# Opening and closing parts of two attention stages over several PSUM banks

## The reference

```
q, k, v = projections of x, 16 heads of 64
scores  = q . k * scale   (+ causal mask in the first, + rel_bias[bucket(key - query)] in the third)
attn    = softmax(scores)
out     = sum over heads of W_O . (attn . v)
x       = layernorm(x + out)
```

## Time and profile before

| what | value |
|---|---|
| median of 3 runs | 4450.3 us (4441.75 to 4450.66) |
| profiled execution | 4442.77 us, its span 4441.0 us |
| TensorE, VectorE, ScalarE, GpSimd busy | 87%, 73%, 43%, 66% of the span |
| mean granted TensorE clock | 0.944 of full |
| s0 with its weights | 0 to 1230 us |
| gated stage | 1233 to 2619 us |
| s2 with its weights | 2623 to 4302 us |
| expert stage | 4305 to 4441 us |

### The profile page before, as it was taken

How to read it: one execution, slowest core, us unless ns; L and a number is a source line. 1 busy time by engine, 2 the same in 40 slices (tenths; PEclk the granted TensorE clock), 3 DMA queues, 4 the chain that set the end, 5 groups by cost and what they waited for, 6 DMA issues and landing times. The chain is left out here.

```text
span 4441.0 us, 63434 instructions
## 1 busy us (share of the span) xinstructions
PE 3881.5 (87%) x22554; PEld 2209.9 (50%) x22554; DVE 3243.7 (73%) x5656; ACT 1923.2 (43%) x3478; POOL 2937.1 (66%) x2164
## 2 busy tenths in 40 slices
PE   5998998999868889889899847999999999999964
PEld 3555555555445555555555423555455445545523
DVE  3786877868577787777876627888788788878826
ACT  1443443444345455455455312444344444434423
POOL 0776775757626777877887833777677677767740
PEclk6999999999979999999999957999999999999987
DMA  3000000000020000100000021122212221212111
GB/s 53 14 14 14 24 14 24 18 6 6 1 75 27 19 28 27 37 19 28 32 28 10 6 62 25 29 38 35 39 29 40 32 40 29 42 24 41 19 53 33
DMA packets 98041, 125.90 MB, mean 28 GB/s; under 512 B 28896, under 2 KB 76448, under 8 KB 97728
## 3 DMA queue, kind: packets, MB, share of 16 engines
q1 hardware_dynamic: 97728, 121.86, 12.5%
HBM read 103.69 MB, written 18.12 MB: 27 GB/s over the span
## 5 line engine op out<-in xcount | busy, mean ns | idle before, releaser
L776 POOL TENSOR_TENSOR s_psum_p<-s_psum_p,s_prob 128x1024 f32<-128x1024 f32 (+3 forms) x640 | 1335.6, 2087 | 388.3 <-ACT s_prob L511 338.3
L511 ACT ACTIVATE s_prob<-s_sT 128x1024 f32<-128x1024 f32 (+2 forms) x896 | 791.6, 931 | 877.2 <-DVE s_sT L658 495.1
L412 PE MATMUL s_pv<-s_prob,s_vp 128*64 128x512 f32 (+3 forms) x3584 | 797.7, 566 | 3.9 <-POOL s_prob L761 3.9
L614 DVE CUSTOM_DVE_ANT_0 s_mx<-s_mx,s_strip 128x512 f32<-128x512 f32 x640 | 429.6, 712 | 177.2 <-PE s_mx L371 174.7
L1670 POOL TENSOR_TENSOR s_psum_p<-s_psum_p,s_prob 128x1024 f32<-128x1024 f32 x192 | 462.1, 2407 | 104.7 <-ACT s_prob L1393 102.6
L1393 ACT ACTIVATE s_prob<-s_sT 128x1024 f32<-128x1024 f32 x256 | 262.4, 1025 | 581.9 <-PE s_sT L1257 581.9
L371 PE MATMUL s_mx<-s_bh,s_ah 64*128 64x512 f32 (+3 forms) x1792 | 412.1, 455 | 110.3 <-DVE s_bm L604 48.3
L663 DVE RECIPROCAL s_recip<-s_recip 128x128 f32<-128x128 f32 x512 | 452.4, 921 | 35.2 <-ACT s_recip L459 35.2
L776 POOL TENSOR_TENSOR s_psum_p<-s_prob 128x1024 f32<-128x1024 f32 (+1 forms) x128 | 288.0, 2250 | 236.2 <-ACT s_prob L511 233.5
L604 DVE TENSOR_REDUCE s_bm<-s_mx 128x8 f32<-128x1024 f32 (+3 forms) x384 | 367.4, 957 | 54.6 <-PE s_mx L371 45.7
L371 PEld LDWEIGHTS s_mx<-s_bh,s_ah 64*128 64x128 f32 x1792 | 171.9, 188 | 466.6 <-issue 192.1
(11 more groups left out here) (251 smaller groups left out, 7395.6 us busy)
## 6 DMA issues: line engine op xcount, KB each, us to landing
s_strip<-bias_rows SPq DMA_DIRECT2D x256, 144.0 KB, 5.7
s_wr<-gated_weights SPq DMA_DIRECT2D x32, 960.0 KB, 4.8
s_near<-bias_rows SPq DMA_DIRECT2D x256, 48.0 KB, 2.0
x<-s_x SPq DMA_DIRECT2D x12, 512.0 KB, 3.2
s_x<-x SPq DMA_DIRECT2D x8, 512.0 KB, 5.1
gated_weights<-s_side_hi SPq DMA_DIRECT2D x8, 480.0 KB, 2.6
gated_weights<-s_side_lo SPq DMA_DIRECT2D x8, 480.0 KB, 2.9
s_x<-in_L_attn_x_dram SPq DMA_DIRECT2D x4, 512.0 KB, 4.3
```

The source lines that it names most:

```text
L412: last = mm(pv[heads(hd), lo:CH], vp[:, g % 2, j, heads(hd)], prob[:, k % PR, hd, lo:CH], start=j == 0, stop=end)
L511: nc.scalar.activation(prob[:, k % PR, :, lo:CH], sT[:, k % 2, :, lo:CH], ACT.Exp, scale=st.scale).then_inc(exp_done, 1)
L614: last = nc.vector.tensor_tensor_reduce(out=mx[:, hd, :], in0=mx[:, hd, :], in1=strip[:, g % 2, hd, first:first + CH], scale=1.0, scalar=N ...
L776: nc.gpsimd.tensor_tensor(out[:, :, lo:CH], src, p[:, :, lo:CH], ALU.add)\
```

## The change

- `bank_of` gives the first jobs banks of their own: xt and v of pair 0 use `misc` and `pv`, the four items of pair 0 the four banks of `sT`; these don't wait for a free `misc`. In the closing y uses two banks of `sT` and t the two others.
- `chunk_bank`: the maxima of pair 0 rotate over `mx` and the two halves of `sT`. TensorE may be three chunks ahead of VectorE.
- The order of the opening: v of pair 0 comes after three maxima, the items of pair 1 after maxima 4, 6, 8 and 10. A first scores job waits until all maxima are read.
- y of the last batch waits for the normalization only before its last pair of heads.
- The closing's layer norm goes in two halves (`half_norm`, `half_scale`, two roots, two stores).
- The x loads of the first two batches are issued in the weights block: in s0 before the bias store, whose landing the block no longer waits for (ScalarE waits for it before copying z of pair 7, and SP at the end of the stage); in s2 before the load of `wo`.
- `recycle` only notes the semaphores; `clear` clears those of the gated stage in the weights block of s2. The blocks that only cleared are gone.

```diff
+        def bank_of(job):
+            kind, of, k = (job + (0,))[:3]
+            if of == 0 and kind in ("xt", "v"):
+                return (misc, pv)[k][:, :]
+            if of == 0 and kind == "item":
+                return sT[:, k // 2, k % 2, :]
+            if of == B - 1 and kind in ("y", "t"):
+                return sT[:, 0 if kind == "y" else 1, k, :]
+            return misc[:, :]
+
+        def chunk_bank(g, n):
+            return mx[:, :, :] if g > 0 or n % 3 == 0 else sT[:, n % 3 - 1, :, :]
...
-                misc_free()
-                before = job
+                out = bank_of(job)
+                if job[0] in ("y", "t") and job[1] == B - 1:
+                    pe.wait_ge(exp_done, GP * U)
+                elif job[0] not in ("xt", "item", "v") or job[1] > 0:
+                    misc_free()
+                    before = job
...
                 elif kind == "y":
-                    if k == 0:
+                    if of < B - 1 and k == 0:
                         pe.wait_ge(z_done, 2 * NPAIR * (of + 1))
                     for p in range(NPAIR):
-                        last = mm(misc[:, :], wo[:, p, :], z[:, (of * NPAIR + p) % NZ, half(k)],
+                        if of == B - 1 and p == NPAIR - 1:
+                            pe.wait_ge(z_done, 2 * GP - 1 + k)
+                        last = mm(out, wo[:, p, :], z[:, (of * NPAIR + p) % NZ, half(k)],
                                   start=p == 0, stop=p == NPAIR - 1)
...
-                pe.wait_ge(mx_read, NMX * g + n)
+                if g > 0:
+                    pe.wait_ge(mx_read, NMX * g + n)
+                elif n >= 3:
+                    pe.wait_ge(mx_read, n - 2)
+                elif n > 0:
+                    pe.wait_ge(lo_done, 2 * n)
...
                 if k >= 2:
                     pe.wait_ge(exp_done, k - 1)
+                else:
+                    pe.wait_ge(mx_read, NMX)
...
-            for k in range(2):
-                misc_job(("v", 0, k))
             for n in range(NMX):
                 maxima(0, n)
-                if n < 4:
-                    misc_job(("item", 1, n))
+                if n == 2:
+                    for k in range(2):
+                        misc_job(("v", 0, k))
+                    pe.wait_ge(v_done, 2)
+                if n in (4, 6, 8, 10):
+                    misc_job(("item", 1, n // 2 - 2))
...
+                if st.causal and s == 2 * (NZ - 2):
+                    act.wait_ge(rows_stored, 16)
...
+            def half_norm(h):
+                part = slice(4 * h, 4 * h + 4)
+                x, square = x2[:, (B - 1) % 2, part, :], yT[:, half(h)].rearrange("p (i d) -> p i d", d=D)
+                mean, var = sums[:, 0, part], sums[:, 1, part]
+                dve.wait_ge(res_done, 2 * (B - 1) + h + 1)
+                nc.vector.tensor_reduce(mean, x, X, ALU.add).then_inc(end_step, 1)
...
+            def half_scale(h):
...
-            for n in range(7):
-                layer_norm(B - 1, n)
+                half_norm(c)
+            for c in range(2):
+                half_scale(c)
...
-            root(B - 1)
+            for h in range(2):
+                root(B - 1 + h, slice(4 * h, 4 * h + 4))
...
-            store(B - 1)
-            sp.wait_ge(x_stored, 16 * B)
+            for h in range(2):
+                sp.wait_ge(end_done, h + 1)
+                sp.dma_start(x_rows(x_out, B - 1)[:, 4 * h:4 * h + 4, :], x2[:, (B - 1) % 2, 4 * h:4 * h + 4, :])\
+                    .then_inc(x_stored, 16)
+            sp.wait_ge(x_stored, 16 * (B + 1))
...
+                for b in range(2):
+                    load(sp, b)
                 sp.wait_ge(b_copied, 4)
                 sp.dma_start(tables, rows.unsqueeze(1).to_broadcast([H, ROWS, TAB])).then_inc(b_stored, 16)
-                sp.wait_ge(b_stored, 16)
             else:
+                for b in range(2):
+                    load(sp, b)
                 sp.dma_start(wo[:, :, :], w["Wo"].rearrange("(t p) d -> p t d", p=P)).then_inc(loaded, 16)
+                cst.clear(sp)
...
     def recycle(self, used):
-        with self.nc.Block() as block:
-            @block.sync
-            def _(sp):
-                for sem in used:
-                    sp.sem_clear(sem)
-        self.spent += used
+        self.pending = used
+
+    def clear(self, sp):
+        for sem in self.pending:
+            sp.sem_clear(sem)
+        self.spent += self.pending
+        self.pending = []
```

More of the change, by code:

```diff
@@ L328, in misc_job @@
                     side, c, cols = 2 * (k // 2), k % 2, slice(p * P, (p + 1) * P)
-                    mm(misc[:, :], wab[:, side, cols], xh[:, half(c)], start=True, stop=False)
-                    mm(misc[:, :], wab[:, side, cols], xl[:, half(c)], start=False, stop=False)
-                    mm(misc[:, :], wab[:, side + 1, cols], xh[:, half(c)], start=False, stop=True)\
+                    mm(out, wab[:, side, cols], xh[:, half(c)], start=True, stop=False)
+                    mm(out, wab[:, side, cols], xl[:, half(c)], start=False, stop=False)
+                    mm(out, wab[:, side + 1, cols], xh[:, half(c)], start=False, stop=True)\
                         .then_inc(ab_full, 1)
@@ L344, in misc_job @@
                     for n in range(4):
-                        last = nc.tensor.transpose(misc[:, n * P:(n + 1) * P], x2[:, of % 2, 4 * k + n, :],
+                        last = nc.tensor.transpose(out[:, n * P:(n + 1) * P], x2[:, of % 2, 4 * k + n, :],
                                                    cst.ident[:, :])
@@ L358, in misc_job @@
                         i = 4 * k + n
-                        last = nc.tensor.transpose(misc[:, n * P:(n + 1) * P], yT[:, i * P:(i + 1) * P],
+                        last = nc.tensor.transpose(out[:, n * P:(n + 1) * P], yT[:, i * P:(i + 1) * P],
                                                    cst.ident[:, :])
@@ L449, in _ @@
             misc_job(("rs", 2 * GP - 1))
[L450 to L453 removed]
+            for kind in ("y", "t"):
+                for c in range(2):
+                    misc_job((kind, B - 1, c))
         @block.scalar
@@ L477, in misc_job @@
                     dst = ah if k < 2 else bh
-                    copy(dst[:, of % 3, half(k % 2)], misc[:, :]).then_inc(hi_done, 1)
+                    copy(dst[:, of % 3, half(k % 2)], src).then_inc(hi_done, 1)
                 elif kind == "v":
@@ L489, in misc_job @@
                         act.wait_ge(v_full, 2 * NPAIR * of)
-                    copy(xh[:, half(k)], misc[:, :]).then_inc(xh_done, 1)
+                    copy(xh[:, half(k)], src).then_inc(xh_done, 1)
                 elif kind == "y":
@@ L495, in misc_job @@
                         act.wait_ge(ln_step, LN * of)
-                    copy(yT[:, half(k)], misc[:, :]).then_inc(yT_done, 1)
+                    copy(yT[:, half(k)], src).then_inc(yT_done, 1)
             def exponentials(k):
@@ L847, in raw_weights @@
                         .then_inc(raw_in, 16)
-            for b in range(2):
-                load(b)
             for g in range(GP):
@@ L1764, in gated_stage, with attention_weights @@
         return used
-def attention_weights(nc, cst, st, w, wab, wv, wo, scratch, sT, bias, banks):
+def attention_weights(nc, cst, st, w, wab, wv, wo, scratch, sT, bias, banks, load):
     with ExitStack() as ctx:
@@ L1864, in _ @@
                     .then_inc(lo_cut, 1)
+    return b_stored if turn else None
 def expert_stage(nc, cst, w, x_in, out):
```

68 lines of the change are left out of this document (42 added, 26 removed).

## The result

| | before | changed kernel |
|---|---|---|
| median | 4450.5 us (4441.8 to 4451.1) | 4350.8 us (4348.2 to 4356.8) |
| span of the profiled execution | 4441.0 us | 4349.2 us |
| mean granted TensorE clock | 0.944 | 0.955 |

The ratio is 0.978, with an interval of 0.9767 to 0.9794: the change makes the kernel 98 us faster (92 to 104). Between the two profiled executions it is 91.8 us, against 89 forecast, and the profiled execution of before was one of its fastest.

The account below looks back on a forecast made before the run. TensorE bounds the long middle of a stage; openings and closings are bound by waits between instructions. Terms 14.5 + 19.6 + 1.5, 8.9, 8.5, 0.9 + 24.5 + 1.5, 8.9 sum to 89 us: 4354 or 4361, predicted 4358, range 4342 to 4382.

Parts of the forecast that it names:

- Start of s0: Before s0's first transpose: without the bias-table wait and with x loaded early, it comes at 23.7 instead of 38.16, gaining 14.5 us.
- Opening of s0: First transpose to pair 0's last maximum in s0: six banks make it 32.5 instead of 52.1 us, gaining 19.6.
- Clock: Openings of s0 and s2: four gapless items may raise TensorE to full clock for v; 0 to 3 us each, 1.5 taken.
- Opening of s2: First transpose to pair 0's last maximum in s2: 38.0 instead of 62.5 us, gaining 24.5, plus 1.5 for the clock.
- Closings: Ends of s0 and s2: earlier y and fewer copy waits bring the first addition 8.1 us earlier; 8.9 each with the store.
- The 1.2 for an earlier rise of the clock: Closings of s0 and s2: TensorE, busy since the rowsum product, reaches full clock sooner in y, saving about 1.2 us.
- Clearing: Between stages: dropping the semaphore-clearing blocks saves 2.5, 3.5 and 2.5 us, sum 8.5; 50 clears cost some 3 us if uncovered.
- Start of s2: s2's weights block: x ahead of wo delays the cast 3.3 us, yet the transpose comes at 2640.4 instead of 2641.39, gaining 0.9.
- Pairs: Steady loop over pairs in s0 and s2: each pair's jobs unchanged, TensorE-bound, so nothing gained or lost.
- covers fail: Rival, 0.15: delays by W_O, strips, clock, root, stores and small stalls cost up to 19 us together; 70 gained, 4377.
- More: Rival, 0.07: both openings at full clock throughout, items also twice as fast (2.5 each); 98 us or more gained, 4344.
- The clock swings between banks: Rival, 0.04: closings over four banks stay at half clock, losing 5.0 each, openings miss 3; 61 us gained, 4386.

Follow-up runs that it names:

- the last run above: Changed kernel with, in s2's opening, x loads behind wo, pair 0's strips issued in the weights block and 17 spare TensorE matmuls: ratio 0.978, median 4351.4 us.

## Why the prediction came out right, and where its steps were off

- **Start of s0**, 14.5: right in size (14.36), right in part in cause. The wait is 10.8, x itself 3.5. W_O did not wait for x: its landing took 7.9 us before and after, and its last cut stands at 22.20 instead of 21.67. That the first transpose is at 23.80 as forecast is in part luck: the weights end 0.5 us later, and the change of blocks takes 0.6 us where I took 1.
- **Opening of s0**, 19.6 + 1.5: it gained 24.3. The step that was off is VectorE's share. I took the 17.3 us of work and *added* 25 gaps; in the rows of the changed kernel most instructions that wait for nothing start 0.08 us before the modelled end of the one before them (a reduction behind the addition of the mask 0.03 after it), so that 17.6 us of durations, added up one by one, cover 16.50 us. In the rows of before, the same durations covered 17.34, since VectorE waited between most of them. Beside v it stood 1.35 us, where 3.9 less the 1.5 for the clock were forecast, and the first maximum came 9.5 instead of 10.2 us after the first transpose, since the four transposes of a half took 0.66 us where the earlier trace rows have 1.09 and the first item started after 2.8 us instead of 3.4. That is 1.6 + 1.1 + 0.7 us, less 0.2 for small waits of 0.5 where 0.3 were forecast: the 3.2 us. The Trainium skill has a rule for the first of these that I had passed over: in "Perfetto Trace Analysis", section "Optimizing Scalar/DVE Operations", the profiled time of an instruction contains the acknowledgement of its writes, which overlaps with the next instruction. The trace agrees in sign, with the 0.08 us of these rows.
- **Clock**, 0 to 3, taken at 1.5 in each opening: the wait beside v is 3.0 us shorter in s0 and 3.1 in s2 behind a gapless run of items than without it; at half clock it was 4.37 in s0, where I had 3.9. I took the middle for want of a row; it was the upper end. That it was so in s0 is in part luck of the execution: of the nine with this opening, three had 0.69 to 0.79 during v and a wait of 2.3 to 2.8 us, which leaves 1.6 to 2.1 for the clock.
- **Opening of s2**, 24.5 + 1.5: it gained 29.75, by the same two steps: 22.18 us of work instead of 24.7, and a stall of 0.64 beside v instead of 3.1 less 1.5.
- **Closings**, 8.1 each to the first addition: 8.06 and 7.60. The largest part, the start of y, was 5.6 against 5.5. The 1.2 for an earlier rise of the clock is not borne out: with the late start put back y took 0.6 and 0.3 us more, less than the 1.7 by which it varies with the early start. The term was too large, and what is left for the copies between the halves, 1.9 and 1.7 where I had 1.4, made up for it in part. The split norm at nothing was right in s0, and the smaller store at 0.8 measured 1.0 and 0.5, norm and store together.
- **Clearing**, 2.5, 3.5 and 2.5: measured 2.6, 4.1 and 2.2 by putting the blocks back. One figure beside this sum is wrong: at the slope between the gaps (1.0 us for 11 clears) 50 clears are 4.5 us and not some 3. In the last run above 3.3 us lie between SP's last issue and VectorE's next row, so the 3 fits better than its derivation.
- **Start of s2**, 0.9: it gained nothing. The term for wo behind x was 3.3, from the bytes at 318 GB/s, with 5 as its upper bound; it was 4.7, with x ahead of it in the queue and SP standing 4.00 us in the issue of wo; how much each of these adds is open. Moving x behind wo gets 3.7 back.
- **Pairs** at nothing: right. Their loops differ by -2.2 and +2.5 us, inside what unchanged code shows, and the early start alone gave nothing back.

Of the rivals, *covers fail* did not come: of its items only the rise of the clock in the closings failed, for the larger part; the landing of wo, late by 1.4 us beyond its term, was not among them. *More* was nearest: its mechanism, the clock at full during v, is there, though not at full throughout: 0.64 in the items of s0. *The clock swings between banks* would have left y at half clock; y took 15.29 us, where 32 steps of 0.86 are 27.5. The Trainium skill's rule on cycling through PSUM banks ("TensorE: Matmul & The Clock Gate", section "A second HAM failure mode: psum-queue depth-cycling") therefore does not describe y here, whose matmuls follow each other without a gap. The times of the rivals are not on one footing: 4377 and 4386 hold the 4 us that lead from the profiled execution of before toward the median, the others don't.

The touched pieces gave 94.9 us instead of 89, 7 more than forecast in the two openings and 1 less elsewhere; the others took 3.1 back. So the profiled execution came at 4350.9 where the sum says 4354. The rest of the way to 4358 is the 4 us that I had added because the runs of before lay at either end of 4442 to 4451; the changed kernel's median, 4350.8, is level with its profiled execution.

## What to carry to other kernels

Give the first and last jobs of a stage the PSUM banks that the steady loop doesn't yet or no longer needs, and put a stock of finished chunks ahead of the longest TensorE job: here this was worth some 50 of the 98 us (31.8 and 18.4 where each was undone alone; both runs also lose the full clock beside v, so its 3 us in each opening stand in both numbers). Place each wait directly before the operation that reads the data (5.6 us in each closing), not at the start of its job or at the end of a block. Before moving a small transfer or a clear under an idle engine, list what is queued in front of it and behind it: three of the four attempts on the start of s2 woke the next wait, and the one that moved a single transfer gained the most there.

## What the runs showed of the hardware beyond what I expected

- The granted clock in the opening of s0 is not the same from run to run for the same code. In the changed kernel it is 1.00 from 33.30 to 38.00; in the run with x behind wo, strips and spare matmuls, whose s0 is the same code, the same stretch has 0.77 and the next 0.50:

```profile
34.29:39.00 4.71, 3.90 (x26) 3.53 (x26) 3.17 (x7) 1.19 (x2) 0.00 (x0) 0.77 0.29 67
39.00:54.09 15.09, 11.39 (x30) 5.62 (x30) 13.42 (x19) 2.39 (x4) 0.00 (x0) 0.50 0.00 1
```

  The piece takes 1.5 us more there (19.80 against 18.33); over nine runs with this code it takes 18.15 to 19.98.
- The recorded clock is not always the one the matmuls ran at: in the run with the early start alone it is 1.00 from 25.13 to 49.00, while the four items take the same 10.80 us as before at 0.50; in the run with the whole norm the items stand at 1.00 with a step of 0.43 us. The readings of the clock beside v rest on stretches in which the matmuls' own lengths agree with it (2.89 and 5.38 us for the v jobs).
- A pause of TensorE between the spare matmuls and x of 1.05 us left the clock at 1.00; with one of 3.73 the transposes behind it still ran at full, 0.66 us for four, and the items at half. After a pause of 1.64 us behind the transposes of the weights, in s0 of the changed kernel, it was the same. These are single stretches, with different work in front of the pause, and no rule is drawn from them.
- SP stood long in a DMA issue where four or five loads of 512 KB had been issued just before: 4.00 us for wo, 4.55 for x in s0, 5.24 where x stood behind wo.
- Small DMAs behind a large one delayed it: eight strips of 144 KB behind wo made it land 3 us later than without them (12.3 us from its issue instead of 9.4).
- The root of 4 columns on GpSimd took 1.04 and 1.38 us.
